# Twenty-five node tiles in the first gather stage, and the first sum of squares formed by TensorE

## The chip, the cores and the metric

The kernel runs on one core of a Trainium2 chip. The metric is the device time of the whole program in microseconds. Engines are named as in the profile: PE (TensorE, with PEld for its weight loads), DVE (VectorE), ACT (ScalarE), POOL (GpSimd, which issues the indirect gathers) and SP (SyncE, which issues the plain transfers).

## The reference

A chain of four graph layers over x (100000 nodes, 64 features) with 25000 edges; after each layer stands a layer norm of x plus the layer's output:

```python
x = _layernorm(x + _L0_gnn_ref(x, ..., src, dst))
x = _layernorm(x + _L1_gnn_ref(x, edge_attr_2, src, dst, ...))
x = _layernorm(x + _L2_gnn_ref(x, edge_index, ...))
x = _layernorm(x + _L3_gnn_ref(x, edge_index, ...))
```

Most nodes receive no edge. For those the layers' outputs are simple: layer 0 gives relu(b_ffn), layer 1 gives zero, layer 2 gives a linear map of the node's own state plus a bias, layer 3 gives zero. So their four norms shrink to a dense path with two sums of squares. The nodes that are some edge's dst need the real sums; they are few, and are written over the dense result at the end.

## The kernel before

**Edges** are sorted by dst and handled in 25 edge tiles of 1024 (NS = 25, SE = 1024; the last has 424 edges in its first half only, so its gather is 4 indirect transfers where the others have 8). A state tile is 128 x 512: two edges' 64 features on the partitions, or one edge row of 8 x 64 on each partition. **Nodes** are handled in 98 node tiles of 1024.

The program is a row of stages, each a block with a barrier at its end. Names as in the code:

- The stage S (setup) and the stage SA (up to about 600 us): gather x by src and dst, dense path for the src states, sums by dst, a lookup.
- S0 (c_, from 601 to 886 us): gather from table[0] (8 indirect transfers for each edge tile, line 461), gate with an exp, segment sum by two scans (lines 472 and 476), ffn matmul (line 1150), norm (lines 491 to 526), and back to features on partitions (line 533). No node tile here.
- S1 (d_, 886 to 1217 us): gather from table[1], moments and logits of layer 1, and beside them the first 50 node tiles, two for each edge tile (`paced`).
- S2, the softmax SF, and S3 (to 1438 us): no gather, no node tile.
- S4 (h_, 1438 to 1717 us): gather from table[2], logits of layer 2, and the other 48 node tiles.
- The softmax SI, S5, and S6 (gather and scatter, to the end).

**Orders.** Each engine's order within a stage is written out by `pipelined` (a slot for each edge tile) or `paced` (two slots for each edge tile, one for each node tile). In slot t, a step of depth d works on tile t - d. Every step is a generator; `yield v` gives it a place in the slot, and `merge` runs the pieces in order of v, older tiles first. So engines are strictly in order: a wait holds everything behind it. GA, GB, XN, W and the PSUM banks P have two halves (par 0 and 1), for even and odd tiles.

**A node tile before** (S1, S4): load from x (line 633), 4 transposes (467), vt = identity plus bias (653, ACT), `dense_pe`: 4 chunks against center and 4 against chain (610), both with nodes on the partitions of the output; Square (616), `dense_sum` (621, DVE: 128x512 to 128x8), sqrt (600), reciprocal (675), y0 (625), bias (627), Square (666), reduce (682), sqrt, reciprocal (685), product (688), store to out_x (638). An f32 matmul is two records in the profile, a transpose is one.

Lines the prediction follows in S0: 1108 product of states (DVE), 1118 V, 472/476 scans, 1150 ffn matmul, 1139 logit matmul, 1111 clip, 517 reduce of the norm, 526 its product, 1123 u, 1158/1166/1161 relu, relu and exp (ACT; exp and sqrt need different tables, so there are two ACT_TABLE_LOAD for each edge tile).

Of the kernel before, what the change touches and what calls it, by code (L numbers as in the profile page):

```python
# [143 lines left out]
def build(nc, a, out):  # L144
    ctx = ExitStack()
    with ctx:
# [354 lines left out]

        def keeping(dve, S):
            for par in range(2):
                dve.sem_inc(S(f"kept{par}"), 1)
# [23 lines left out]
        def back_dve(dve, T, s, par, k, step=1):  # L528
            yield step
            dve.wait_ge(T("x_fm"), k)  # L530


            dve.scalar_tensor_tensor(at(XD, s), at(MORE, s), 0.0, P[4 * par + 3][:, ::-1], A.is_equal, A.mult).then_inc(T("kept"), 1)
# [57 lines left out]

        def sm(par, k, n=1):
# [54 lines left out]
        def node_pe1(pe, T, n, par, k):  # L647
            yield from dense_pe(pe, T, par, k, 0)
# [22 lines left out]
        def node_dve2(dve, T, n, par, k):  # L671
            yield from dense_sum(dve, T, par, k, 0)
# [30 lines left out]
        def only(base, *stages):  # L703

            def of_node(stage):
                return lambda T, n, par, k: stage(T, n, par, k) if is_node(n, base) else None
            return [stage and of_node(stage) for stage in stages]

        def nodes_sync(sp, S, base, *owns):
# [12 lines left out]
            paced(sp, S, only(base, load, None, None, None, None, store), owns)  # L722
            count = min(NODES, NG + 1 - base)
            for par in range(2):
                sp.wait_ge(S(f"out_stored{par}"), 16 * ((count + 1 - par) // 2 + 1))

        def nodes_tensor(pe, S, base, *owns, unrolled=False):
            for par in range(2):
                pe.sem_inc(S(f"xn_free{par}"), 1)
            paced(pe, S, only(base, None, partial(node_pe0, pe), partial(node_pe1, pe)), owns, unrolled)  # L730

        def nodes_scalar(act, S, base, *owns):
            paced(act, S, only(base, None, partial(node_act0, act), partial(node_act1, act), partial(node_act2, act), partial(node_act3, act)), owns)

        def nodes_vector(dve, S, base, *owns):
            paced(dve, S, only(base, None, None, None, partial(node_dve2, dve), partial(node_dve3, dve)), owns)
# [361 lines left out]
        S0 = Sems("c_")  # L1098
        with nc.Block() as block:
# [5 lines left out]
            def _(dve):  # L1105
                def gate(T, s, par, k):
# [4 lines left out]
                    dve.tensor_scalar(W[par][2], P[4 * par + 1][:, :], -5.0, 5.0, A.max, A.min).then_inc(T("clipped"), 1)  # L1111

                def sums(T, s, par, k):
# [9 lines left out]
                    dve.tensor_tensor(W[par][4], at(XD, s), W[par][3], A.add).then_inc(T("u"), 1)  # L1123
                keeping(dve, S0)
                pipelined(dve, S0, gate, sums, partial(norm_dve, dve), partial(back_dve, dve))

# [655 lines left out]
```

## Time and profile before

| | before |
|---|---|
| median of 3 runs (range) | 2573.97 us (2572.82 to 2577.59) |
| profiled execution, whole / span | 2577.51 / 2575.7 us |
| mean granted TensorE clock | 0.748 |
| busy share PE, PEld, DVE | 54%, 32%, 73% |
| busy share ACT, POOL | 31%, 55% |

The span runs from the first to the last instruction. The granted clock is a share of 2.4 GHz: 1.0 is 2.4 GHz and 0.5 is 1.2 GHz. A busy share over the whole span mixes the stages, which have different limits, so the views below are cut by stage.

### The profile page before, as it was taken

The page shows a single profiled execution, that of the slowest core. Times are in us where ns is not written, and L with a number is a line of the kernel's source. Part 1 is how long each engine was busy: PE and PEld are TensorE (multiplying, and loading weights), DVE is VectorE, ACT ScalarE, POOL GpSimd, SP SyncE. Part 2 cuts the span into 40 slices and gives each one's busy share as a digit, 9 for nine tenths or more (in the row PEclk, how much of TensorE's full clock was granted, in tenths as well). Part 3 has the DMA queues.
Part 4 walks back from the last instruction along what each step waited for, and adds up shares of the span by engine and source line. Part 5 has one row for each costly group of instructions (what it writes and reads, how often), then busy time and mean ns, then how long its engine had stood idle before and what let it go on. Part 6 is the DMA issues. An engine that isn't in the chain of part 4 may idle for free. (4 is left out here: it accounts for less than half of the span.)

```text
span 2575.7 us, 25825 instructions
## 1 busy us (share of the span) xinstructions
PE 1392.9 (54%) x5738; PEld 832.2 (32%) x5738; DVE 1867.6 (73%) x3900; ACT 791.9 (31%) x1636; POOL 1423.4 (55%) x1382
## 2 busy tenths in 40 slices
PE   1433444444666588887466577634888543333231
PEld 1332333331333354443233455421333221212120
DVE  3877777875767589998688699977888675455542
ACT  1222222222545355554122355531222110101010
POOL 6777777735777576662000577730000277777776
PEclk9656555555877699999688899976888666566666
DMA  5433333431111233332011244420000011101010
GB/s 176 119 110 108 110 104 98 119 91 33 52 44 49 58 102 106 108 105 74 20 39 39 87 128 127 127 78 16 31 27 27 28 23 23 25 23 24 22 22 13
DMA packets 120400, 174.79 MB, mean 68 GB/s; under 512 B 36128, under 2 KB 42382, under 8 KB 120340
## 3 DMA queue, kind: packets, MB, share of 16 engines
q1 hardware_dynamic: 74836, 129.98, 15.0%
q0 software_dynamic: 43904, 43.81, 8.6%
q10 hardware_dynamic: 1600, 0.33, 0.1%
q8 instruction: 22, 0.36, 0.1%
q14 instruction: 38, 0.31, 0.0%
HBM read 88.48 MB, written 86.74 MB: 68 GB/s over the span
## 5 line engine op out<-in xcount | busy, mean ns | idle before, releaser
L461 POOL DMA_INDIRECT GA<-table,look_i x588 | 608.0, 1034 | 493.5 <-PEq L1473 213.0
L467 PE MATMUL P<-ident,GA 128*128 128x128 f32 x500 | 105.3, 348 | 411.6 <-DMA GB<-in_x,dst_i 198.9
L491 PE MATMUL P<-center,work 128*128 128x128 f32 x800 | 152.1, 352 | 210.9 <-DVE work L1697 174.2
L266 POOL DMA_INDIRECT GA<-in_x,src_i x196 | 210.6, 1074 | 83.5 <-issue 70.8
L1637 POOL DMA_INDIRECT out_x<-work,seg_i x196 | 205.0, 1046 | 59.8 <-issue 59.5
L1629 POOL DMA_INDIRECT GA<-table,look_i x196 | 200.2, 1022 | 59.8 <-issue 59.4
L266 POOL DMA_INDIRECT GB<-in_x,dst_i x196 | 196.9, 1004 | 59.7 <-issue 59.7
L509 ACT ACTIVATE work<-P 128x512 f32<-128x512 f32 x100 | 59.7, 597 | 518.6 <-PE P L491 518.1
L491 PEld LDWEIGHTS P<-center,work 128*128 128x128 f32 x800 | 135.9, 257 | 242.2 <-issue 113.1
L467 PEld LDWEIGHTS P<-ident,GA 128*128 128x128 f32 x500 | 71.1, 176 | 441.7 <-issue 222.3
L610 PE MATMUL P<-center,work 128*128 128x128 f32 x984 | 160.6, 313 | 91.1 <-ACT work L653 67.4
L610 PEld LDWEIGHTS P<-center,work 128*128 128x128 f32 x984 | 136.2, 215 | 169.7 <-ACT work L653 96.5
L1641 POOL MEMSET GA<- 128x512 f32 x1 | 0.5, 524 | 339.7 <-SPq L1622 339.7
L610 PE MATMUL P<-chain,work 128*128 128x128 f32 x984 | 146.4, 298 | 0.0
L1003 DVE SCALAR_TENSOR_TENSOR work<-P,src_f,unit_row 128x200 bf16<-128x200 f32 x400 | 142.5, 422 | 0.4
L610 PEld LDWEIGHTS P<-chain,work 128*128 128x128 f32 x984 | 136.4, 215 | 0.0
L566 DVE TENSOR_TENSOR_SCAN work<-MORE,car,XD 64x512 f32 (+1 forms) x100 | 127.9, 1279 | 8.2 <-DVEq L556 0.7
L908 PE MATMUL P<-step_up,work 128*128 128x201 bf16 x400 | 72.7, 358 | 102.6 <-DVE work L1003 98.2
L517 DVE TENSOR_REDUCE small<-work 128x8 f32<-128x512 f32 x100 | 68.4, 684 | 73.7 <-ACT work L509 72.9
L467 PE MATMUL P<-ident,work 128*128 128x128 f32 x400 | 81.9, 342 | 68.9 <-DVE work L526 67.0
L1599 PE MATMUL P<-work,wh 128*128 128x512 f32 x200 | 114.9, 713 | 1.5
L600 ACT ACTIVATE small<-small,vec 128x8 f32<-128x8 f32 x221 | 65.1, 295 | 141.8 <-DVE small L682 123.4
(332 smaller groups left out, 3448.9 us busy)
## 6 DMA issues: line engine op xcount, KB each, us to landing
table<-work SPq DMA_DIRECT2D x175, 256.0 KB, 2.4
XN<-in_x SPq DMA_DIRECT2D x98, 256.0 KB, 2.7
out_x<-work SPq DMA_DIRECT2D x98, 256.0 KB, 2.4
GA<-table,look_i POOLq DMA_INDIRECT x784, 2.4
XN<-in_src_pad SPq DMA_DIRECT2D x13, 512.0 KB
cols<-in_dst_pad SPq DMA_DIRECT2D x50, 128.5 KB, 4.7
table<-XN SPq DMA_DIRECT2D x1, 6400.0 KB
src_wide<-in_src_pad SPq DMA_DIRECT2D x12, 512.0 KB, 5.4
```

What stands on the lines that cost most here:

```text
L266: pool.indirect_dma_start(buf[:, s % 2, j * D:(j + 1) * D], None, a["x"], bass.IndirectOffsetOnAxis(ap=look[:, s * 8 + j:s * 8 + j + 1], a ...
L461: pool.indirect_dma_start(GA[:, par, j * D:(j + 1) * D], None, table_k, bass.IndirectOffsetOnAxis(ap=look[:, s * 8 + j:s * 8 + j + 1], axis=0)
L467: ins = pe.transpose(dst[:, q * 128:(q + 1) * 128], src[:, q * 128:(q + 1) * 128], ident[:, :])
L491: ins = pe.matmul(norm_bank(par, far)[:, q * 128:(q + 1) * 128], W[par][4][:, q * 128:(q + 1) * 128], center[:, :], start=True, stop=True)
L517: dve.tensor_reduce(small[:, par, 0:8], rows(W[par][5]), AX, A.add).then_inc(T("variance"), 1)
L566: dve.tensor_tensor_scan(B[lo:hi, ::-1], more, x, car[lo:hi, :], A.mult, A.add).then_inc(S(f"back{h}"), 1)
L610: ins = pe.matmul(p[:, q * 128:(q + 1) * 128], VT[:, q * 128:(q + 1) * 128], w[:, :], start=True, stop=True)
L908: ins = pe.matmul(block_of(par, q), steps(par)[:, h * HW + q * 128:h * HW + (q + 1) * 128], step_up[:, part, 0:RC + 1], start=(part == 0), ...
L1003: ins = dve.scalar_tensor_tensor(W[par][spare].bitcast(BF16)[:, q * RC:(q + 1) * RC], block_of(par, q)[:, 0:RC], src_f[:, col], unit_row[: ...
L1599: pe.matmul(P[4 * par][:, :], wh[g][:, :], W[par][g], start=(g == 0), stop=(g == HEADS - 1)).then_inc(T("head_sum"), 1)
L1629: pool.indirect_dma_start(GA[:, par, j * D:(j + 1) * D], None, table[3], bass.IndirectOffsetOnAxis(ap=look_i[:, r * 8 + j:r * 8 + j + 1], ...
L1637: pool.indirect_dma_start(out, bass.IndirectOffsetOnAxis(ap=seg_i[:, r * 8 + j:r * 8 + j + 1], axis=0), W[par][6][:, j * D:(j + 1) * D], N ...
```

## The change

1. **25 node tiles move to S0.** Node tiles 1, 3, ..., 49 are done in S0, one beside each edge tile. In S1 `even=True` keeps only the even ones of the first 50 (the odd steps aren't issued). S4 keeps its 48.
2. **Banks are shared in S0.** The gate has P[1] for both parities (its first matmul waits until the tile before has been clipped), the transposes back have P[3] for both; P[5] and P[7] are the node tiles' NA and NB. Node states are in XN (NX) and GB (NV).
3. **The first sum of squares, for all 98 node tiles.** The center matmul has center as its weights and the 512 columns of vt as the moving side: features on partitions. Square goes over that. `row_sums` then takes each chunk of 128 columns of the squares as weights and two columns of `total` as the moving side: 4 matmuls, 8 sums on each partition, in PSUM, where ACT's sqrt reads them. The DVE reduce of line 621 is gone for node tiles.
4. **In S0 new steps on each queue**: SP a load at the slot's start, which waits for `node_ss1` of two tiles before, and a store at place 4; ACT's `node_start` waits for `node_stored`.

```diff
+        def row_sums(pe, dst, squares):
+            for q in range(4):
+                ins = pe.matmul(dst[:, 2 * q:2 * q + 2], squares[:, q * 128:(q + 1) * 128], total[:, 0:128:64], start=True, stop=True)
+            return ins
         def node_pe1(pe, T, n, par, k):
-            yield from dense_pe(pe, T, par, k, 0)
+            VT = W[par][0]
+            yield 0
+            pe.wait_ge(T("vt"), k)
+            if not (isinstance(k, int) and k == 1):
+                pe.wait_ge(T("y0"), k - 1)
+            pe.matmul(BN[par][1], center[:, :], VT, start=True, stop=True).then_inc(T("dense_mm"), 1)
+            for q in range(4):
+                ins = pe.matmul(BN[par][2][:, q * 128:(q + 1) * 128], VT[:, q * 128:(q + 1) * 128], chain[:, :], start=True, stop=True)
+            ins.then_inc(T("dense_mm"), 1)
+        def node_pe2(pe, T, n, par, k):
+            yield 0
+            pe.wait_ge(T("sq1"), k)
+            row_sums(pe, BN[par][1], W[par][1]).then_inc(T("ss1"), 1)
         def node_act2(act, T, n, par, k):
             yield 1
             act.wait_ge(T("ss1"), k)
-            double_root(act, T, par, 2, 0, "sd1")
+            act.activation(sm(par, 2), BN[par][1][:, 0:8], ACT.Sqrt, scale=(1.0 + EPS) / D, bias=eps_2).then_inc(T("sd1"), 1)
         def node_dve2(dve, T, n, par, k):
-            yield from dense_sum(dve, T, par, k, 0)
             yield 2
...
+                def node_first(T, s, par, k):          # S0, DVE, with the norm of tile s
+                    yield 5
+                    dve.wait_ge(T("node_sd1"), k)
+                    dve.reciprocal(sm(par, 4), sm(par, 4)).then_inc(T("node_r1"), 1)
...
+                    dve.tensor_tensor(rows(NV[par]), rows(NB), per_row(sm(par, 4)), A.mult).then_inc(T("node_y0"), 1)
...
+                                      A.add).then_inc(T("node_y"), 1)
+                def node_second(T, s, par, k):         # S0, DVE, with the way back of tile s
+                    yield 1
+                    dve.wait_ge(T("node_sq2"), k)
+                    dve.tensor_reduce(sm(par, 5), rows(W[par][5]), AX, A.add).then_inc(T("node_ss2"), 1)
+                    yield 3
...
+                    dve.tensor_tensor(rows(NV[par]), rows(NV[par]), per_row(sm(par, 6)), A.mult).then_inc(T("node_out"), 1)
...
+                def node_turn(T, s, par, k):           # S0, PE
+                    yield 5
+                    pe.wait_ge(T("node_x"), 16 * k)
...
+                        pe.wait_ge(S0(f"node_sd1{older}"), turn)
+                    transpose4(pe, NA, NX[par]).then_inc(T("node_xt"), 1)
+                def node_dense(T, s, par, k):
+                    yield 1
...
+                    pe.wait_ge(T("node_vt"), k)
...
+                    pe.matmul(NA, center[:, :], NV[par], start=True, stop=True)
+                    for q in range(4):
+                        ins = pe.matmul(NB[:, q * 128:(q + 1) * 128], NV[par][:, q * 128:(q + 1) * 128], chain[:, :], start=True, stop=True)
+                    ins.then_inc(T("node_mm"), 1)
+                    yield 4
+                    pe.wait_ge(T("node_sq1"), k)
+                    row_sums(pe, NA, NX[par]).then_inc(T("node_ss1"), 1)
...
+                def node_start(T, s, par, k):          # S0, ACT, with the sums of tile s
+                    yield 6
+                    act.wait_ge(T("node_xt"), k)
+                    act.wait_ge(T("node_stored"), 16 * k)
+                    act.activation(NV[par], NA, ACT.Identity, bias=relub).then_inc(T("node_vt"), 1)
+                def node_first(T, s, par, k):          # ACT: Square at 2, sqrt of node_ss1 at 4
...
+                def node_second(T, s, par, k):         # ACT: Square of y at 0, sqrt of node_ss2 at 2
...
+                def node_load(T, s, par, k):           # S0, SP, depth 0
+                    yield 0
+                    if not (isinstance(k, int) and k == 1):
+                        sp.wait_ge(T("node_ss1"), k - 1)
+                    sp.dma_start(NX[par], rows_of(a["x"], (2 * s + 1) * SE)).then_inc(T("node_x"), 16)
+                def node_store(T, s, par, k):          # depth 3
+                    yield 4
+                    sp.wait_ge(T("node_out"), k)
+                    sp.dma_start(rows_of(out, (2 * s + 1) * SE), NV[par]).then_inc(T("node_stored"), 16)
```

(The words behind # in the diff are put in here to say where a step stands.)

## Rows read from the trace of the kernel before

**Rows 1.** Windows by stage (S0, S1, S4): length, busy PE, PEld, DVE, ACT, POOL, clock, DMA, GB/s.
```profile
610.00:875.00 265.00, 170.60 (x528) 88.15 (x528) 184.64 (x287) 129.34 (x166) 196.05 (x190) 0.77 0.18 46
890.00:1215.00 325.00, 268.63 (x1349) 154.76 (x1348) 282.18 (x549) 187.07 (x476) 201.88 (x194) 0.97 0.35 101
1438.00:1706.00 268.00, 185.04 (x1156) 130.65 (x1156) 238.91 (x429) 143.65 (x309) 200.92 (x196) 0.97 0.43 121
```

**Rows 2.** Groups by line, S0 from 620 to 860 us: busy, mean ns, idle before.
```profile
L461 POOL DMA_INDIRECT GA<-table,look_i x178 | 184.4, 1036 | 56.0 <-issue 56.0
...
L1118 DVE TENSOR_TENSOR work<-P,work 128x512 f32<-128x512 f32 x22 | 15.2, 692 | 38.9 <-PE P L467 38.9
```

**Rows 3.** Groups by line, S1 from 900 to 1200 us.
```profile
L461 POOL DMA_INDIRECT GA<-table,look_i x186 | 195.1, 1049 | 85.2 <-issue 51.6 <-PEq L1223 33.6
...
L610 PE MATMUL P<-center,work 128*128 128x128 f32 x384 | 56.6, 292 | 29.5 <-ACT work L653 22.5 <-PE P L1245 6.9
...
L621 DVE TENSOR_REDUCE small<-work 128x8 f32<-128x512 f32 x48 | 32.7, 681 | 0.0
...
L653 ACT ACTIVATE work<-P,vec 128x512 f32<-128x512 f32 x48 | 32.5, 677 | 0.0
...
L666 ACT ACTIVATE work<-work 128x512 f32<-128x512 f32 x47 | 29.4, 626 | 0.0
```

**Rows 4.** Groups by line, S4 from 1450 to 1690 us.
```profile
L461 POOL DMA_INDIRECT GA<-table,look_i x180 | 184.0, 1022 | 56.2 <-issue 56.2
...
L610 PE MATMUL P<-center,work 128*128 128x128 f32 x360 | 52.7, 291 | 43.5 <-ACT work L653 41.5 <-PE P L467 1.8
```

**Rows 5.** All of line 1118: min/median/max ns, first and last start.
```profile
L1118 DVE TENSOR_TENSOR work<-P,work x25: 690/692/693, 614.5 to 871.6; 128x512 f32<-128x512 f32 x25
```

**Rows 6.** Timeline, PE: first and last transposes of a gathered tile, S1, then S4.
```profile
898.60 1.12 PE L467 MATMUL P<-ident,GA 128*128 128x128 f32 x4 [3.02 <-DMA GA<-table,look_i]
...
1197.58 0.63 PE L467 MATMUL P<-ident,GA 128*128 128x128 f32 x4 [0.30 <-PE P L467]
...
1451.40 0.90 PE L467 MATMUL P<-ident,GA 128*128 128x128 f32 x3 [4.04 <-DMA GA<-table,look_i]
...
1702.62 0.66 PE L467 MATMUL P<-ident,GA 128*128 128x128 f32 x4 [0.84 <-DMA GA<-table,look_i]
```

**Rows 7.** Timeline, one slot of S0: start, length, engine.
```profile
740.58 0.68 DVE L1108 TENSOR_TENSOR work<-XS,XD 128x512 f32 x1
...
741.18 0.68 DVE L533 SCALAR_TENSOR_TENSOR XD<-MORE,P 128x512 f32 x1
...
742.76 0.69 DVE L1118 TENSOR_TENSOR work<-P,work 128x512 f32<-128x512 f32 x1 [0.90 <-PE P L467]
...
746.53 1.79 PE L1150 MATMUL P<-work,wffn 128*128 128x512 f32 x2 [2.63 <-DVE work L476]
...
746.69 0.69 DVE L517 TENSOR_REDUCE small<-work 128x8 f32<-128x512 f32 x1
...
750.06 0.69 DVE L1111 TENSOR_SCALAR work<-P 128x512 f32<-128x512 f32 x1 [0.30 <-PE P L1139]
```

**Rows 8.** Timeline of S1: a node tile on DVE, and a 512-column matmul at full clock.
```profile
1024.45 0.19 DVE L675 RECIPROCAL small<-small 128x8 f32<-128x8 f32 x1
...
1024.67 0.69 DVE L625 TENSOR_TENSOR work<-P,small 128x512 f32<-128x512 f32 x1
...
1025.40 0.69 DVE L627 TENSOR_TENSOR work<-work,bias_row 128x512 f32<-128x512 f32 x1
...
1029.39 1.10 PE L1231 MATMUL P<-XS,wfc 128*128 128x512 f32 x2
```

**Rows 9.** Line 1034, two stores of 256 KB one after the other: issue (ns), landing (us).
```profile
L1034 SPq DMA_DIRECT2D table<-work x50: 332/377/450, 77.1 to 580.2; - x50
...
DMA to landing us min/median/max: 2.1/2.8/3.4
```

**Rows 10.** Line 1380, the two records of one matmul with two moving columns: min/median/max ns.
```profile
L1380 PE MATMUL P<-red,fold x2: 355/365/375, 1219.5 to 1219.7; 128*128 128x2 f32 x2
```

More of the change, by code:

```diff
@@ L701, in first_of, with only, nodes_sync @@
             return N - SE if is_last(n, base) else (n + base) * SE
-        def only(base, *stages):
+        def only(base, *stages, even=False):
             def of_node(stage):
-                return lambda T, n, par, k: stage(T, n, par, k) if is_node(n, base) else None
+                return lambda T, n, par, k: stage(T, n, par, k) if is_node(n, base) and not (even and par) else None
             return [stage and of_node(stage) for stage in stages]
-        def nodes_sync(sp, S, base, *owns):
+        def nodes_sync(sp, S, base, *owns, even=False):
             def load(T, n, par, k):
@@ L1098, in build, with tile_before @@
         S0 = Sems("c_")
+        NX, NV = ([g[:, par, :] for par in range(2)] for g in (XN, GB))
+        NA, NB = P[5][:, :], P[7][:, :]
+        def tile_before(par, k):
+            return 1 - par, k - 1 + par
         with nc.Block() as block:
@@ L1132, in gate @@
                 def gate(T, s, par, k):
-                    bank = P[4 * par + 1][:, :]
+                    bank = P[1][:, :]
                     yield 1
                     pe.wait_ge(T("product"), k)
+                    if not (isinstance(s, int) and s == 0):
+                        older, turn = tile_before(par, k)
+                        pe.wait_ge(S0(f"clipped{older}"), turn)
                     pe.matmul(bank, proj[:, :], W[par][0], start=True, stop=True).then_inc(T("cos"), 1)
@@ L1157, in gate @@
                     act.wait_ge(T("cos"), k)
-                    act.activation(W[par][1], P[4 * par + 1][:, :], ACT.Relu, scale=inv_scale).then_inc(T("relu"), 1)
+                    act.activation(W[par][1], P[1][:, :], ACT.Relu, scale=inv_scale).then_inc(T("relu"), 1)
                     yield 5
@@ new lines, in node_second @@
+                def node_second(T, s, par, k):
+                    yield 0
+                    act.wait_ge(T("node_y"), k)
+                    act.wait_ge(T("variance"), k)
+                    act.activation(W[par][5], NV[par], ACT.Square).then_inc(T("node_sq2"), 1)
+                    yield 2
+                    act.wait_ge(T("node_ss2"), k)
+                    act.activation(sm(par, 6), sm(par, 5), ACT.Sqrt, scale=(1.0 + EPS) / D, bias=eps_2).then_inc(T("node_sd2"), 1)
+                pipelined(act, S0, gate, together(sums, node_start), together(partial(norm_act, act), node_first), node_second)
@@ L1171, in _ @@
                 storing(sp, S0)
-                pipelined(sp, S0, None, None, lambda T, s, par, k: store_table(sp, T, table[1], s, par, k, 6))
+                for par in range(2):
+                    sp.sem_inc(S0(f"node_stored{par}"), 16)
+                pipelined(sp, S0, node_load, None, lambda T, s, par, k: store_table(sp, T, table[1], s, par, k, 6), node_store)
                 all_stored(sp, S0)
+                sp.wait_ge(S0("node_stored0"), 16 * (NS // 2 + 2))
+                sp.wait_ge(S0("node_stored1"), 16 * (NS // 2 + 1))
```

58 lines of the change are left out of this document (40 added, 18 removed).

## The prediction

> **What bounds the kernel now.** A share over the whole span says little here, so I read the stages first [rows 1], then the groups by line within the three that change. In S0 the gathers set the pace: POOL's idle time in 240 us is all "issue", the short pause between two gathers, and there is no wait for a buffer; a gather and its pause take (184.4 + 56.0)/178 = 1.35 us [rows 2]. DVE waits there: 38.9 us for the transposes of the gathered tile [rows 2]. From the first V to the last, 24 edge tiles take 871.6 - 614.5 = 257.1 us, 10.71 each [rows 5]. S4 is the same, (184.0 + 56.2)/180 = 1.33 us a gather and nothing else in POOL's idle time [rows 4]; from the first to the last transposes (1702.6 - 1451.3)/24 = 10.47 us a tile (the last tile has half the gathers) [rows 6]. S1 is different: POOL waits 33.6 us until PE has freed a buffer [rows 3], and a tile takes (1197.58 - 898.60)/24 = 12.46 us [rows 6]; DVE is busy 282 of 325 us, head and tail included, and PE 269 [rows 1]. So S1 has two node tiles too much for the pace of its gathers, and S0 has room: 185 of 265 us on DVE, 171 on PE.
>
> **S1, what is taken away.** A node tile costs DVE two reduces, y0, bias and product, and two reciprocals: 5 x 0.69 + 2 x 0.2 = 3.85 us, by 0.68 us for a reduce [rows 3] and 0.69 and 0.19 us for the others [rows 8]. One of the two goes, and the other loses its reduce: 4.5 of 12.46 us, leaving about 8. PE loses a node tile: its center part is 56.6/48 = 1.18 us [rows 3], chain the same, transposes half, so 3 us. For the other, center becomes one matmul of 512 columns, 1.10 us [rows 8] for 1.18, and row_sums is added. Its price is not in the trace in this form. Bounds: the eight chunk records of center take 1.18 us with 128 moving columns each, and less can't be more, so 1.2 is the upper end at full clock; the two records with two moving columns took 0.36 us each, overlapping, at half clock [rows 10], so eight would be 1.6 us there and 0.8 at full clock. I take 0.8 to 0.9, by the row of the same shape; the lower end is nothing, if the loads hide under other matmuls. PE has then about 9.5 us of work for an edge tile, from 268.6/25 = 10.7 [rows 1]. Both are under the gathers' pace, so S1 falls to what S4 shows, 10.47 us: 24 x (12.46 - 10.47) = **-48 us**. If PE's waits add up to 11 us a tile it is -35.
>
> **S4.** Its gathers bound it and 48 reduces less on DVE (33 us of work) bring nothing. PE gets 1.7 us more for an edge tile, on 185/25 = 7.4 [rows 1]; but it waits 41.5 us, nearly 2 us a tile, for vt before the center matmul [rows 4], and row_sums stands right before that wait and needs only the Square that ACT does before vt. So it fills a wait: **+1 us**, between -2 and +12.
>
> **S0, what is added on DVE.** Per edge tile: reciprocal, y0, bias, reduce, reciprocal, product. Operations that don't hang on each other start 0.60 us apart (740.58 to 741.18 [rows 7]), dependent ones 0.73 (1024.67 to 1025.40), a reciprocal and its follower 0.22 [rows 8]. Slot by slot the new order is: product 0.60, way back 0.60, node reduce 0.65, V to the ffn matmul 3.77 (742.76 to 746.53 [rows 7]), copy 0.16, reduce 0.62, node reciprocal and product 0.84, norm's reciprocal and product 0.88, u 0.61, clip 0.61, then node reciprocal, y0 and bias 1.56: 10.9 us. That alone would be 0.2 over the gathers' 10.7, nearly free.
>
> **S0, the wait that is added.** SP is in order. Its load for tile t waits for row_sums of tile t - 2, which PE reaches late in slot t, behind ffn and logit. Behind that load stands the store of tile t - 3, whose data has been ready since the product. And ACT's node_start in the same slot waits for that store to have landed, since it writes the same buffer; behind it on ACT stands the Square of y, for which DVE waits (the node reduce) before it may go on to V and the scans; and PE's ffn matmul needs the scans. That is a ring once round per slot:
> - row_sums done to load issued 0.2, its issue 0.4, store's issue begins 0.1 later; landing 2.8 us from there (2.1 to 3.4 for a pair of such stores [rows 9]): 3.5 us.
> - Identity 0.68 and Square 0.63 [rows 3], overlapping by 0.1, and the hand-over to DVE: 1.2 us.
> - node reduce to V 0.65, V to ffn 3.77: 4.4 us.
> - ffn and logit: 2.0 us at full clock (1.10 for one [rows 8], and the next begins before its end), row_sums 0.85, end of the last 0.15: 3.0 us.
> The sum is 12.1 us. At half clock ffn to clip takes 750.06 - 746.53 = 3.53 us [rows 7] and the ring is some 1.5 longer. PE's clock in S0 is 0.77 now [rows 1], and it falls when PE has waited through the scans, for 2.63 us [rows 7]; after the change PE has the node matmuls in front of the scans and waits about 1.9 us, so I take one slot in ten slow: **12.2 us** a tile. It holds for 22 intervals (before slot 3 no store is waited for): 22 x (12.2 - 10.7) = +33 us. At the end the last node tile runs its own chain behind the norm's center matmul: center and chain 2, Square 0.6, row_sums 0.9, root 0.3, three DVE steps 1.6, Square, reduce, root and product 2.3, store and landing 3.2, 11 us; the norm's own Square, reduce, root, product and store need some 5 from the same point, and vt comes a microsecond or two late. So the 27.0 us from the last V to S1's first transposes (871.6 to 898.6 [rows 5, 6]) grow by **+8 us**, an estimate. S0 together **+41 us**, from +13 (at 11.0 us) to +75 (at 13.7).
>
> ACT gets about 2.5 us for each tile on 129/25 = 5.2 [rows 1], none of it a new table load, since the new roots stand beside the old one and ahead of the exp; it is covered but for the ring. The shared gate bank waits for a clip that is a slot old: nothing. Gathers would run ahead of DVE and wait for buffers: nothing.
>
> **A rule against it.** Gathers keep 1.35 us each with DVE 70% busy in S0 and 1.33 with DVE 89% busy in S4 [rows 1, 2, 4]; DVE's work doesn't slow them, so S4's rate is used for S1. The Trainium skill (SBUF — State Buffer, Who interferes with whom) says that GpSimd and VectorE share a port pair as an exclusive lock, so gathers' descriptors can be held up by VectorE; by that rule S0 would lose more and S1 and S4 gain; the trace doesn't bear it out.
>
> **Sum.** -48 + 1 + 41 = -6 us. Profiled execution 2577.5 -> 2571.5; it lay 3.5 above the median, so against the median 2573.97 the forecast is 2568 us.
>
> **Rivals.**
> A. *The ring is longer: the clock.* If PE waits a little more than 1.9 us before ffn, it drops to half clock in most slots, as it does now in S0: ring 13.4 us, S0 22 x 2.7 + 8 = +67, net +20: 2594 us. It decides from a ring of about 13 us on. For it: clock 0.77 now, and a late landing (3.4 us) adds to it. Against: PE gets 4 us more work a slot.
> B. *The ring is hidden.* If the store lands early or SP's load isn't late, DVE's order bounds S0 at 11.1 us: +9 + 6 = +15, net -32: 2542 us. Against it is the order of SP's queue; for it, that each term is at most a tenth of a microsecond off only if nothing overlaps, and some may.
> C. *PE bounds S1 and S4.* row_sums at 1.2 us or more, with waits: S1 11.0, S4 10.9 us a tile: 41 - 35 + 10 = +16: 2590 us. For it: PE was 83% busy in S1. Against: it fills waits.
> D. *Gathers get faster where DVE is relieved.* If a gather and its pause took 1.25 us, S1 and S4 would lose 16 us more each: -38: 2536 us. The three stages' rates speak against it. (The rule of the Trainium skill's page above would give this.)
>
> **Chances.** Forecast 0.42 (its own range 2559 to 2577), A 0.20, B 0.15, C 0.13, D 0.04, something else (0.06, spread evenly). Between 2545 and 2596 lie the forecast, most of A and C, and the upper edge of B; what is left out is most of B, D and the far end of A, 0.19. A difference of 0.2%, 5 us, is about what a measurement of this kernel can tell from none. Faster by more than that: 0.23 of the forecast's, B, D and 0.01 of the rest, 0.43; within it 0.15 of the forecast's and 0.08 of A, C and the rest, 0.23; slower 0.34.
>
> **What would show it.** V (line 1118's successor) in S0 12.2 us apart, ACT's Identity in S0 held by the landing of the store, DVE's node reduce held by ACT; POOL in S0 with waits for buffers and in S1 without; S1's gathered transposes 10.5 us apart and S4's unchanged; S0's clock above 0.85; row_sums 0.8 to 0.9 us. If S0's pace is 11 us, the ring was mis-seen; if S1's is over 11, PE was.

## The result, and where the time went

| | before | after |
|---|---|---|
| median of 4 runs (range) | 2575.43 us (2572.82 to 2577.59) | 2623.74 us (2618.76 to 2629.97) |
| ratio, 95% interval | | 1.0185 [1.0165, 1.0205] |
| profiled execution, whole / span | 2577.51 / 2575.7 us | 2618.76 / 2616.9 us |
| mean granted TensorE clock | 0.748 | 0.753 |

The changed kernel is 1.85% slower; 2568 us were forecast, with 2596 as the upper end. Between the two spans lie 41.2 us; the medians lie 48.3 apart, since the profiled execution of before was the slowest of its four and that of after the fastest. The marks that the prediction named cut up the 41.2: the product V of S0 (line 1118 before, 1149 after), and the transposes of the gathered tiles.

```profile
L1149 DVE TENSOR_TENSOR work<-P,work x25: 678/680/692, 615.9 to 921.2; 128x512 f32<-128x512 f32 x25
...
954.16 1.11 PE L467 MATMUL P<-ident,GA 128*128 128x128 f32 x4 [3.37 <-DMA GA<-table,look_i]
...
1217.62 0.60 PE L467 MATMUL P<-ident,GA 128*128 128x128 f32 x4
...
1471.84 1.11 PE L467 MATMUL P<-ident,GA 128*128 128x128 f32 x4 [3.53 <-DMA GA<-table,look_i]
...
1745.44 0.63 PE L467 MATMUL P<-ident,GA 128*128 128x128 f32 x4
```

(All of line 1149 with its first and last start; then, in time, the first and last transposes of a gathered tile in S1 and in S4, of after.) Against [rows 5, 6]:

| stretch | before | after | difference | forecast |
|---|---|---|---|---|
| start to the first V | 614.5 | 615.9 | +1.4 | 0 |
| S0, first V to last | 257.1 (10.71 a tile) | 305.3 (12.72) | +48.2 | +33 |
| last V to S1's first transposes | 27.0 | 33.0 | +6.0 | +8 |
| S1, first transposes to last | 299.0 (12.46) | 263.5 (10.98) | -35.5 | -48 |
| to S4's first transposes | 253.8 | 254.2 | +0.4 | 0 |
| S4, first to last | 251.2 (10.47) | 273.6 (11.40) | +22.4 | +1 |
| the rest | | | -1.7 | 0 |

Three terms missed, all to the same side: S0 by 15 us, S1 by 12, S4 by 21. The last lies outside the forecast's bounds for it (-2 to +12) and is twice the 10 us that rival C had.

**S0 in the profile of after.** The ring that the prediction walked through is there. (A ring: each wait in it is ended by the one before, so that a turn takes the sum of its members.) One turn at full clock, from one ffn matmul to the next (start, length, engine; in brackets the idle time before and what ended it):

```profile
759.47 1.13 PE L1205 MATMUL P<-work,wffn 128*128 128x512 f32 x2 [1.97 <-DVE work L476]
...
761.29 0.95 PE L601 MATMUL P<-total,XN 128*128 128x2 f32 x8
...
762.52 0.35 SPq L1275 DMA_DIRECT2D XN<-in_x  x1
...
763.17 0.33 SPq L1280 DMA_DIRECT2D out_x<-GB  x1
...
766.41 0.69 ACT L1249 ACTIVATE GB<-P,vec 128x512 f32<-128x512 f32 x1 [1.92 <-DMA out_x<-GB]
...
767.65 0.69 DVE L1169 TENSOR_REDUCE small<-work 128x8 f32<-128x512 f32 x1 [1.56 <-ACT work L1263]
768.25 0.68 DVE L1149 TENSOR_TENSOR work<-P,work 128x512 f32<-128x512 f32 x1
...
774.50 1.70 PE L601 MATMUL P<-total,XN 128*128 128x2 f32 x8
```

The row sums end at 762.24, SP issues the load and then the store, ACT's bias waits until the store has landed, DVE's reduce waits for ACT, V for the reduce, and the next ffn starts at 771.97: 12.5 us. The last line is the row sums of the next turn, at half clock: 1.70 us for 0.95, and that turn takes 13.6 us. Grouped by line over 280 us of S0:

```profile
L461 POOL DMA_INDIRECT GA<-table,look_i x184 | 192.7, 1047 | 88.7 <-issue 53.6 <-PEq L1202 35.1
...
L1249 ACT ACTIVATE GB<-P,vec 128x512 f32<-128x512 f32 x22 | 15.1, 686 | 32.6 <-DMA out_x<-GB 32.6
...
L1169 DVE TENSOR_REDUCE small<-work 128x8 f32<-128x512 f32 x21 | 14.4, 685 | 31.7 <-ACT work L1263 31.7
```

POOL now waits 35.1 us for buffers, where it waited for none [rows 2]: the gathers have lost the lead to the ring.

**S4 in the profile of after.** Here POOL waits for nothing, before and after. The gathers themselves have become longer, 1145 ns for 1022 [rows 4]:

```profile
L461 POOL DMA_INDIRECT GA<-table,look_i x179 | 205.0, 1145 | 56.2 <-issue 56.2
```

The shortest gathers take 0.94 us, with a pause of 0.30 to 0.31 us, 1.25 together. I call **lost** what the 196 gathers of a stage take above 0.94 us each (184.2 us together). These are the windows around the gathers of S0, S1 and S4 (stretch, its length, POOL busy in gathers (number), clock, share of the DMA engines, GB/s), first of before:

```profile
601.60:865.40 263.80, 202.48 (x196) 0.76 0.18 46
886.60:1179.20 292.60, 204.59 (x196) 0.96 0.37 105
1438.80:1700.60 261.80, 200.92 (x196) 0.97 0.43 122
```

and of after:

```profile
603.20:900.20 297.00, 204.74 (x196) 0.86 0.29 78
942.80:1208.70 265.90, 204.97 (x196) 0.92 0.28 73
1458.80:1742.90 284.10, 222.85 (x196) 0.92 0.40 113
```

S4 lost 16.7 us before and 38.6 after; the window grew by 22.3 us, busy time by 21.9. In both, length less busy time is 61 us, the pauses. What holds a gather is beside it in the timeline of S4. DVE and POOL, after:

```profile
1602.56 0.69 DVE L639 TENSOR_TENSOR work<-work,bias_row 128x512 f32<-128x512 f32 x1
...
1602.68 1.40 POOL L461 DMA_INDIRECT GA<-table,look_i  x1 [0.30 <-issue]
...
1604.12 1.28 DVE L572 TENSOR_TENSOR_SCAN work<-MORE,car,XD 64x512 f32 x1
...
1604.38 1.79 POOL L461 DMA_INDIRECT GA<-table,look_i  x1 [0.30 <-issue]
...
1605.73 1.27 DVE L572 TENSOR_TENSOR_SCAN work<-MORE,car,XD 64x512 f32 x1
...
1606.48 1.30 POOL L461 DMA_INDIRECT GA<-table,look_i  x1 [0.30 <-issue]
```

and before, where the kernel has a reduce ahead of the scans:

```profile
1520.78 0.68 DVE L621 TENSOR_REDUCE small<-work 128x8 f32<-128x512 f32 x1
1521.49 1.28 DVE L566 TENSOR_TENSOR_SCAN work<-MORE,car,XD 64x512 f32 x1
...
1523.11 1.28 DVE L566 TENSOR_TENSOR_SCAN work<-MORE,car,XD 64x512 f32 x1
```
```profile
1522.46 1.08 POOL L461 DMA_INDIRECT GA<-table,look_i  x1 [0.30 <-issue]
1523.85 1.31 POOL L461 DMA_INDIRECT GA<-table,look_i  x1 [0.30 <-issue]
```

A gather that begins while DVE is inside one of these instructions ends 0.8 us after it: 1602.56 + 0.69 = 1603.25, and the gather ends at 1604.08; the scan ends at 1605.40, the gather at 1606.17; the next at 1607.00 and 1607.78; before, the scan at 1522.77 and the gather at 1523.54. What is lost depends on how early in DVE's instruction the gather begins: 0.26 us behind the scan's start costs 0.85 us, 0.97 us behind it 0.14. After the change the bias addition pushes the train of gathers so that the next begins right behind the scan's start. Over the whole stage, counted by the DVE instruction under way when each gather of 1 us or more began, scans held 46 gathers for 12.2 us before and 46 for 25.7 after; the bias addition and the other product held 11 for 2.3 us before and 40 for 11.4 after.

The theory: S0 is the ring; S4 is gathers held back by DVE instructions with two inputs in SBUF, and the change moved only the moments at which they meet. Rivals: S0's added work, S4's PE (rival C of the prediction), or something that the first stages leave for S4.

### The profile page after: what moved, and what is told of

The parts are those of the page before. It is cut to its first block and busy times, and to the rows that moved or that the text cites. A ratio compares the mean times of both kernels' runs of the same rounds, so it can differ in the third digit from the quotient of the medians.

```text
span 2616.9 us, 26206 instructions
## 1 busy us (share of the span) xinstructions
PE 1477.6 (56%) x5934; PEld 886.9 (34%) x5934; DVE 1811.9 (69%) x3802; ACT 796.1 (30%) x1636; POOL 1450.0 (55%) x1382
## 5 line engine op out<-in xcount | busy, mean ns | idle before, releaser
L461 POOL DMA_INDIRECT GA<-table,look_i x588 | 632.6, 1076 | 521.4 <-PEq L1587 215.2
L491 PE MATMUL P<-center,work 128*128 128x128 f32 x800 | 153.0, 353 | 217.0 <-DVE work L1811 178.5
L1743 POOL DMA_INDIRECT GA<-table,look_i x196 | 200.0, 1021 | 59.8 <-issue 59.4
L491 PEld LDWEIGHTS P<-center,work 128*128 128x128 f32 x800 | 136.8, 258 | 244.1 <-issue 117.7
L472 DVE TENSOR_TENSOR_SCAN work<-SAME,car,work 64x512 f32<-64x512 f32 (+1 forms) x75 | 95.8, 1277 | 13.4 <-DVE work L1552 9.1
L476 DVE TENSOR_TENSOR_SCAN work<-SAME,car,work 64x512 f32<-64x512 f32 (+1 forms) x75 | 96.3, 1284 | 8.2
L667 PEld LDWEIGHTS P<-chain,work 128*128 128x128 f32 x584 | 85.5, 211 | 39.9 <-issue 39.9
L665 PE MATMUL P<-work,center 128*128 128x512 f32 x146 | 88.9, 693 | 16.4 <-ACT work L678 9.3
L526 DVE RECIPROCAL small<-small 128x8 f32<-128x8 f32 x100 | 19.7, 197 | 109.7 <-ACT small L518 108.9
```

The lines of the kernel that those rows point to most:

```text
L461: pool.indirect_dma_start(GA[:, par, j * D:(j + 1) * D], None, table_k, bass.IndirectOffsetOnAxis(ap=look[:, s * 8 + j:s * 8 + j + 1], axis=0)
L472: dve.tensor_tensor_scan(F[0:64, :], m[0:64, :], V[0:64, :], car[0:64, :], op0, op1).then_inc(T("scan0"), 1)
L476: dve.tensor_tensor_scan(F[64:128, :], m[64:128, :], V[64:128, :], car[64:128, :], op0, op1).then_inc(T("scan1"), 1)
L491: ins = pe.matmul(norm_bank(par, far)[:, q * 128:(q + 1) * 128], W[par][4][:, q * 128:(q + 1) * 128], center[:, :], start=True, stop=True)
L665: pe.matmul(BN[par][1], center[:, :], VT, start=True, stop=True).then_inc(T("dense_mm"), 1)
L1743: pool.indirect_dma_start(GA[:, par, j * D:(j + 1) * D], None, table[3], bass.IndirectOffsetOnAxis(ap=look_i[:, r * 8 + j:r * 8 + j + 1], ...
```

## The experiments

Ratios are against the kernel before on the same chip; its median was 2579 us beside e1 to e4 and e5 to e7, and 2580 beside e8 to e10. us a tile is over 24 intervals, from the marks above; lost is POOL's, as defined. Both come from one profiled execution of each kernel, which lay up to 7.4 us from its kernel's median (e3's was the fastest of eight, e8's the slowest of four).

| | median us | ratio, 95% interval | S0, S1, S4 us a tile | lost S0, S1, S4 |
|---|---|---|---|---|
| before | 2575.4 | | 10.71, 12.46, 10.47 | 18, 20, 17 |
| after | 2623.7 | 1.0185 [1.0165, 1.0205] | 12.72, 10.98, 11.40 | 20, 21, 39 |
| e1_s4_old | 2598.9 | 1.0089 [1.0065, 1.0112] | 12.56, 10.95, 10.47 | 21, 21, 17 |
| e2_load_late | 2576.5 | 0.9993 [0.9982, 1.0004] | 11.00, 10.81, 11.40 | 21, 20, 38 |
| e3_both | 2557.0 | 0.9923 [0.9903, 0.9943] | 10.98, 10.96, 10.57 | 21, 23, 19 |
| e4_moved_only | 2591.0 | 1.0055 [1.0036, 1.0074] | 12.54, 10.90, 10.47 | 27, 22, 17 |
| e5_sums_only | 2610.0 | 1.0120 [1.0097, 1.0143] | 10.63, 12.92, 11.52 | 16, 27, 40 |
| e6_idle_reduce | 2558.4 | 0.9919 [0.9890, 0.9948] | 10.99, 10.98, 10.58 | 21, 24, 17 |
| e7_moved_late | 2566.7 | 0.9952 [0.9933, 0.9971] | 11.45, 10.97, 10.54 | 31, 24, 18 |
| e8_sums_s0_only | 2552.8 | 0.9893 [0.9873, 0.9912] | 11.21, 10.89, 10.54 | 27, 22, 17 |
| e9_scan_psum | 2558.7 | 0.9920 [0.9902, 0.9938] | 11.23, 11.00, 10.46 | 14, 24, 17 |
| e10_bias_psum | 2545.3 | 0.9859 [0.9834, 0.9883] | 11.31, 10.47, 10.68 | 11, 11, 22 |

### e1_s4_old: S4's sums back on DVE

```diff
-nodes_tensor(pe, S4, NODES, (2, states), (3, logits))
+nodes_tensor(pe, S4, NODES, (2, states), (3, logits), old=True)
```

With old=True the stages on PE, ACT and DVE are dense_pe, double_root and dense_sum, as in the kernel before.

> The changed kernel with one part undone: in S4 alone the node tiles are as before (eight centring and chain matmuls with rows on partitions, the first sum of squares by a DVE reduce, none by PE). Theory (S4's +22.3 us comes from POOL's gathers being held longer once the sums have left DVE and its two-SBUF-input instructions stand at other moments): the interval between S4's gathered transposes returns from 11.40 us to 10.5, POOL's mean gather there from 1145 ns to 1020 to 1050, the time is 2600 us (2597 to 2606). Rival (S4 is slower because of something that the first stages left, or the clock in that stage): S4 stays at 11.3 to 11.4 us a tile and the time at 2618 to 2628.

```profile
1458.10:1719.70 261.60, 200.76 (x196) 0.97 0.43 122
```

S4's window is that of before to 0.2 us, though all that precedes it is as in the changed kernel; the median fell by 24.8 us. So S4's loss comes from how S4's own node tiles are summed, and not from what the first stages leave.

### e2_load_late: the ring opened

```diff
 def node_load(T, s, par, k):
-    yield 0
+    yield 5
```

> The changed kernel, but in S0 SP issues the load of a node tile's rows behind the store of the tile three older (place 5 in its slot, not 0), so the store no longer stands behind a load that waits for row sums. Theory (the ring row sums, load issue, store issue, landing, ACT bias, matmuls, squares, row sums sets S0's 12.7 us): S0's interval falls to 10.9 to 11.4 us, its 24 intervals by 32 to 44 us, ACT's wait for the output store (32.6 us in 280) goes nearly to nothing, the time is 2584 us (2578 to 2594). Rival 1 (the added work on PE and DVE makes S0 longer, the wait only shows it): 12.5 to 12.7 us a tile, 2618 to 2626. Rival 2 (the ring closes again through the late load and PE's transposes of it): 12.0 to 12.5 us a tile, 2605 to 2618.

The gathers' window in S0, and ACT's bias grouped over 620 to 870 us:

```profile
601.90:870.00 268.10, 205.66 (x196) 0.95 0.33 90
```
```profile
L1249 ACT ACTIVATE GB<-P,vec 128x512 f32<-128x512 f32 x23 | 15.4, 669 | 0.0
```

The wait for the store is gone, 32.6 us to nothing, and S0 is 41 us shorter for one changed place in SP's order; no work was taken away. Length less busy time is 62 us, so POOL waits for no buffer. DVE hardly waits either: 3.2 us in the 220 from 640 to 860 us, where it waited 54 in the kernel before. Most intervals between two V are 10.76 and 10.94 us, which is the gathers' pace (8 x 1.25 us and what they lose) and DVE's own order at once. The clock in this window is 0.95, 0.86 in after. The median fell by 47.3 us, to just under my range; the 41 us of the intervals lie in theirs.

### e3_both: the two together

(Both diffs.)

> The two edits together: S0's load behind the store, and S4's node tiles as before. S1 keeps sums by PE. Theory: the two gains add, S0 -36 and S4 -22 to -24 against the changed kernel, which gives 2564 us (2556 to 2574), faster than the kernel before by 0.4%. Rival (the stages are not independent, a gain in one is given back in the next): above 2580.

The gains add to within their scatter: 66.7 us against 47.3 + 24.8 = 72.1 (the intervals of these ratios are 0.1 to 0.2% wide to each side, 3 to 6 us). This kernel is faster than before by 0.8%.

### e4_moved_only: 25 tiles moved, no sums by PE

```diff
-    pe.matmul(NA, center[:, :], NV[par], start=True, stop=True)
+    for q in range(4):
+        pe.matmul(NA[:, q * 128:(q + 1) * 128], NV[par][:, q * 128:(q + 1) * 128], center[:, :], start=True, stop=True)
...
-    row_sums(pe, NA, NX[par]).then_inc(T("node_ss1"), 1)
+    dve.tensor_reduce(sm(par, 3), rows(NX[par]), AX, A.add).then_inc(T("node_ss1"), 1)
```

(In S0; S1 and S4 as S4 in e1.)

> 25 node tiles in S0 as in the changed kernel, but every first sum of squares by a DVE reduce from rows on partitions, in S0, S1 and S4 (one half of the change alone). The load stays ahead of the store in S0. Theory: S4 as in the kernel before, 10.5 us a tile (-22 us against the changed kernel); S0 keeps the ring, with a reduce of 0.6 to 0.7 us and its queueing on DVE in the place of row sums of 1.2 us: 12.2 to 13.0 us a tile; S1 10.3 to 10.6 us a tile if PE's row sums held it at 10.98, which gives 2588 us (2578 to 2605). Rival (S1's missing gain is due to POOL or to PE's other work, and not to the row sums): S1 stays at 10.9 to 11.0, the time is 2600 (2592 to 2612).

The total lies in the range, the theory's part on S1 fell: S1 stays at 10.90 us a tile without a single row sum on PE, so PE's row sums do not hold it there. POOL does: in this window too length less busy time is the pauses alone, and the rest is lost time.

```profile
937.00:1204.30 267.30, 206.39 (x196) 0.94 0.28 73
```

### e5_sums_only: the sums by PE in the kernel before

```diff
-paced(pe, S, only(base, None, partial(node_pe0, pe), partial(node_pe1, pe)), owns, unrolled)
+paced(pe, S, only(base, None, partial(node_pe0, pe), partial(node_pe1, pe), partial(node_pe2, pe)), owns, unrolled)
...
 def node_dve2(dve, T, n, par, k):
-    yield from dense_sum(dve, T, par, k, 0)
```

(With node_pe1, node_pe2 and node_act2 as in after, in S1 and S4.)

> The other half of the change alone: the kernel before with the first sum of squares of every node tile in S1 and S4 by PE, and no node tile in S0. Theory: S4 as in the changed kernel, 11.4 us a tile (+22 us); S1, with 49 node tiles, loses 0.69 us of DVE work for each of two node tiles a slot and gains 1.1 us of PE work for each, 12.46 us a tile becoming 12.2 to 12.7; the time 2595 us (2586 to 2606). Rival (the slow S4 comes from the node tiles moved ahead, that is from the state the first stages leave): S4 10.5 us a tile, 2568 to 2580.

Windows of S1 and S4:

```profile
887.00:1189.20 302.20, 211.35 (x196) 0.97 0.37 102
1450.30:1735.50 285.20, 223.88 (x196) 0.91 0.39 112
```

S4 has the changed kernel's loss (40 us lost) with nothing moved. S1 came out worse than I expected, by 11 us and not 0: 6.8 us of its window are longer gathers (211.35 for 204.59), the other 3 are about what POOL's waits for a buffer that PE frees have grown by (37.1 us for 33.6). The time, 2610, is above my range. By itself, the half of the change that moves work from DVE to PE costs 1.2%.

### e6_idle_reduce: more work on DVE

On e2, in S4 alone; the reduced column is read by nobody, the sums used are PE's.

```diff
 def node_dve2_idle(dve, T, n, par, k):
+    yield 0
+    dve.wait_ge(T("sq1"), k)
+    dve.tensor_reduce(sm(par, 7), rows(W[par][1]), AX, A.add).then_inc(T("idle"), 1)
     yield from node_dve2(dve, T, n, par, k)
```

> The kernel e2_load_late (2576.5 us) with one instruction more a node tile in S4: DVE waits for the squares and reduces them into a column that nobody reads, at the place where the kernel before formed its sum; PE's row sums stay and are what is used. It adds 0.69 us of DVE work to each of 50 tiles. Theory (S4's +22 us is where DVE's two-SBUF-input instructions fall against POOL's gathers, and DVE's schedule decides that): S4's interval goes from 11.41 us to 10.5 to 10.8, the time to 2558 us (2553 to 2565), faster by adding work. Rival 1 (PE's row sums and what waits for them hold S4): 11.4 us a tile, 2573 to 2582. Rival 2 (DVE is short of time there): 11.6 to 12.0 us, 2582 to 2592.

```profile
1415.20:1678.20 263.00, 201.00 (x196) 0.96 0.43 121
```

The trace has 48 of these reduces (not 50), of 0.68 us, and the kernel is 18 us faster than e2: S4's gathers lose 16.8 us, as before the change. PE's row sums are all still there, so they are not the cause (rival C for S4 falls), nor was DVE short of time. A reduce in that place keeps the instructions on both its sides where they do little harm: counted as above, scans hold gathers for 11.9 us where they held 25.6 in e2, and products for 2.3 where they held 10.8.

### m1_beside and m2_spread: the price by itself

Kernels of their own, which compute nothing of the reference: gathers by POOL, and DVE with one kind of instruction.

> A kernel of its own that computes nothing of the reference: nine phases of 32 gathers each by POOL (128 rows of 64 floats by an index column, as in the stages), with DVE idle, or running one kind of instruction throughout: a product of two SBUF tiles 128x512; the same with one input in PSUM; a reduce 128x512 to 128x8; a scan 64x512 with byte mask and values in SBUF; a scan with values in PSUM; a scaling of one SBUF tile; and last the product of two SBUF tiles and the SBUF scan, each followed by a pause as long as an ACT copy. Theory (a gather cannot be finished by POOL while DVE runs an instruction with two inputs in SBUF): alone 0.94 us, reduce and PSUM inputs below 1.05 us, two SBUF inputs without pause 1.3 us or more, the SBUF scan 1.5 us or more, the paused ones between. Rival (DVE's instructions have no part in it): all phases within 5% of the first.

Windows of two of its phases, the products of two SBUF tiles and the scans from SBUF, without pauses between them:

```profile
51.50:91.60 40.10, 30.19 (x32) 1.00 0.14 26
187.50:238.30 50.80, 40.90 (x32) 1.00 0.11 20
```

Both fell short of what was expected. The scans' phase has 40.90/32 = 1.28 us a gather, for 1.5 or more; the scans ended 13 us before the phase did, and the 22 gathers that began beside them took 1.43 us on average, half of them 0.94 and most of the others 1.93 to 1.98. The product cost nothing (30.19/32 = 0.943 us), for 1.3 or more. But two products took 1.25 us, and so did a gather with its pause: each gather began 0.60 us into a product, 0.08 us before its end. In the last two phases, with a pause behind each instruction, the products did hold gathers (20 of them took 1.02 to 1.06 us) and the scans held each that began beside them (1.40 to 1.64 us). Hence the second kernel, with pauses of changing length.

> Again 48 gathers a phase beside one kind of DVE instruction, now with a pause after each that ACT makes, of another length every time, so that gathers and instructions meet at every phase and not at one that repeats (in m1_beside both had a period of 1.25 us in some phases). Phases in order: POOL alone; product of two SBUF tiles; product with one input in PSUM; reduce; scan with byte mask and values in SBUF; scan with values in PSUM; scaling of one SBUF tile; ACT copies alone. Theory (a DVE instruction whose data inputs all come from SBUF holds back the gather that has just begun, until it ends, and 0.76 us more pass then; scans are the worst because they are the longest): mean gather 0.94 us alone and beside ACT, 0.94 to 0.96 beside the reduce and both PSUM forms, 1.03 to 1.15 beside the SBUF product, 1.15 to 1.35 beside the SBUF scan, 0.97 to 1.05 beside the scaling. Rival (only the scan with a byte mask does it, the product of two SBUF tiles does not, as its first phase in m1_beside seemed to say): product 0.94 to 0.96 us.

All eight phases, in the order given there (POOL busy, 48 gathers):

```profile
6.00:66.20 60.20, 45.42 (x48) 1.00 0.14 26
73.00:136.20 63.20, 48.15 (x48) 1.00 0.13 25
143.00:203.00 60.00, 45.29 (x48) 1.00 0.14 26
209.00:269.30 60.30, 45.27 (x48) 1.00 0.14 26
276.00:351.50 75.50, 60.88 (x48) 1.00 0.11 21
358.00:418.00 60.00, 45.28 (x48) 1.00 0.14 26
424.00:486.40 62.40, 47.08 (x48) 1.00 0.13 25
493.00:553.00 60.00, 45.28 (x48) 1.00 0.14 26
```

Divided by 48: alone 0.946 us, product of two SBUF tiles 1.003, product with PSUM 0.944, reduce 0.943, scan from SBUF 1.268, scan with values in PSUM 0.943, scaling of an SBUF tile 0.981, ACT alone 0.943. Two SBUF tiles or an SBUF scan hold gathers, and so does a scaling, 0.45 us long; with one of two inputs in PSUM, nothing does. The product's mean is below my range (1.03 to 1.15): only 7 of the 48 gathers were held, the longest for 1.44 us, and beside the products alone (54 of the phase's 63 us) the mean is 1.013. The scans held all 34 gathers that began while they ran, so their phase doesn't show every meeting either. One meeting in the phase of the scans:

```profile
280.46 1.28 DVE L60 TENSOR_TENSOR_SCAN O<-mask,zero,b_in 64x512 f32<-64x512 uint8 x1 [0.43 <-ACT Q L94]
281.09 1.40 POOL L71 DMA_INDIRECT G<-in_x,idx  x1 [0.30 <-issue]
```

The scan ends at 281.74, the gather at 282.49, 0.75 us later. The Trainium skill (SBUF — State Buffer, Who interferes with whom) has this as an exclusive lock on a port pair that GpSimd shares with VectorE, and says that a reduce never contends: the reduce's row agrees. It says as well that a VectorE instruction with two inputs in SBUF contends with a GpSimd instruction that reads SBUF, yet infers that such a product doesn't hold back the generation of descriptors; 48.15 for 45.3 us here says that it holds an indirect gather back.

### e7_moved_late and e8_sums_s0_only: where are sums by PE worth it?

e7 is e4 with S0's load late, e8 is e3 with S1's sums on DVE too. They differ in S0's sums alone.

> e4_moved_only (2591.0 us: 25 node tiles in S0, every first sum by a DVE reduce) with S0's load behind the store. Theory (the ring was the whole loss of S0, and the sums by PE bring nothing to either stage): S0 11.0 us a tile or less, S1 10.9, S4 10.5, the time 2550 us (2542 to 2558), as good as e3_both's 2557 or better. Rival (in S0 the sums by PE are worth their 0.69 us of DVE a tile): S0 11.5 to 11.7 us a tile, 2560 to 2570.

> e3_both (2557 us) with S1's node tiles as before too, so that PE forms the sums in S0 alone. Theory (S1 runs at the speed of POOL's gathers, 244 us and what they lose, whoever forms the sums): S1 10.9 to 11.0 us a tile and the whole within 5 us of e3_both, 2552 to 2562. Rival (the reduces give S1 more gathers held back, or DVE becomes late there): S1 11.3 us a tile or more, 2565 to 2575.

e8 came as expected, within 5 us of e3 by the medians. e7 did not: S0 takes 11.45 us a tile and the whole 2567 us, as its rival had it (11.5 to 11.7, 2560 to 2570). S0's windows, e7 and then e8:

```profile
598.20:874.60 276.40, 215.04 (x196) 0.90 0.32 87
```
```profile
599.30:872.40 273.10, 210.80 (x196) 0.93 0.32 88
```

Length less busy time is 61 and 62 us in both, so POOL waits for no buffer; e7's gathers lose 31 us and e8's 27, e3's 21 with the same S0 as e8. But gathers alone don't explain e7. This is the larger of the only two waits of DVE in e7 from 640 to 860 us (us in total, times, longest), the other is 0.3 us:

```profile
DVE work L1161 <- PE P L467: 1.6, 2, 1.1
```

DVE works through its order without a wait, and 18 of the 24 intervals are 11.35 to 11.49 us, 0.6 more than the 10.76 and 10.94 of e2 and e3: that is the reduce, which starts 0.6 us ahead of the next instruction. So in S0 DVE is short of time, and the sums by PE are worth their reduce there, as the rival said. In e8 14 of the 24 intervals are 11.4 to 11.9 us, and DVE waits 7.3 us in the same stretch, 5.8 of them for gathered tiles; there the meeting of gathers and DVE does decide, and it varies by some 6 us between the executions of e3 and e8, which are equal in S0. Of the 14 us between the medians of e7 and e8 these profiles show 6 in S0; the rest was not traced.

### e9_scan_psum and e10_bias_psum: operands moved to PSUM

```diff
-V, F = W[par][8], W[par][7]
+V, F = P[4 * par], W[par][7]
...
-dve.tensor_tensor(rows(Y), rows(BN[par][2]), per_row(sm(par, 2)), A.mult).then_inc(T("y0"), 1)
+dve.tensor_tensor(rows(BN[par][2]), rows(BN[par][2]), per_row(sm(par, 2)), A.mult).then_inc(T("y0"), 1)
...
-dve.tensor_tensor(rows(Y), rows(Y), bias_row...
+dve.tensor_tensor(rows(Y), rows(BN[par][2]), bias_row...
```

The first two lines are e9, in S0. The others are e10, which has e9's too; in S0 it does the same to NB, and PE waits for y where it waited for y0.

> e3_both (2557 us) with one operand of S0 moved: the product that feeds the segment scan is written over its own PSUM bank and the scan reads it there, not from SBUF. The same instructions in the same order, of the same sizes. Theory (in S0 too POOL's gathers set the pace: 245 us and the 21 us that they lose, 15 of them to scans from SBUF): the gathers lose 6 to 9 us, S0's interval goes from 10.98 us to 10.3 to 10.5, the time to 2544 us (2538 to 2550). Rival 1 (DVE's own chain is as long and takes over): 10.8 to 11.0 us, 2552 to 2562. Rival 2 (PSUM makes the product or the scan longer): above 2562.

> e9_scan_psum with one operand more moved in every stage that has node tiles: the first product of a node tile stays in its PSUM bank and the bias is added from there, so this addition has one SBUF input and not two; PE gets the bank back one instruction later. Theory: the gathers lose 2 to 3 us less in each of four stretches, 5 to 10 us in all: 2536 us (2530 to 2545). Rival (the bank that comes back later is what is then late, or the phase of the other instructions shifts to a worse place): 2545 to 2560.

S0 of e9: the group of the gathers, and all engines over 240 us (busy PE, PEld, DVE, ACT, POOL, then clock, DMA, GB/s):

```profile
L461 POOL DMA_INDIRECT GA<-table,look_i x177 | 179.7, 1015 | 61.1 <-issue 55.0 <-PEq L1214 6.1
```
```profile
620.00:860.00 240.00, 189.80 (x940) 129.23 (x938) 218.51 (x379) 161.59 (x256) 179.08 (x177) 0.92 0.34 92
```

Not one gather of S0 is held by a scan any more in e9 (in e3 scans held 14.8 us, counted by the DVE instruction under way when each long gather began), which is the mechanism shown in place. But products hold 13.1 us where they held 5.7, POOL has begun to wait for buffers, and DVE is busy 91% of the time. The median lies in the range of rival 1; S0's interval, 11.23 us, lies above all ranges. Fourteen of the 24 intervals are 10.72 to 10.91 us, DVE's own order, as rival 1 said. Six are 12.2 to 13.5 us, and in them the granted clock was down (0.66 over one of 13.4 us, 0.86 over one of 12.2, 1.00 in one of 10.9), so that S0's gathers stood at a clock of 0.89 on average where e3 had 0.95. Whether the lower clock made these intervals long or followed from their waits was not tried. e10's median, 2545.3 us, lies on the border between its range and its rival's. It pays off in S1, where it was not expected to be large:

```profile
900.60:1156.60 256.00, 195.05 (x196) 0.95 0.29 76
1403.60:1670.70 267.10, 205.81 (x196) 0.95 0.42 119
```

S1's gathers lose 11 us for 24 in e9, none of it to the bias addition any more, and its tile takes 10.47 us; S4 loses 4 us more than in e9. At 2545 us, 1.4% under the kernel before, it is the fastest of all; how much of that is luck in how the instructions meet in S1 was not tried.

## Why the prediction was wrong, step by step

**What bounds the stages**: right for S0, S1 and S4 of before. Wrong was what POOL's pace is. I read 1.35 and 1.33 us for a gather and its pause [rows 2, 4] as its speed; it is 1.25 us and 17 to 20 us a stage of meetings with DVE. The mean looked constant because the losses were alike, and not because they were none.

**S4 (+1 forecast, +22.4)**: "row_sums fills a wait" is right, e6 keeps it and has the old time. The step that failed is the one sentence that 48 reduces less on DVE "bring nothing". They were no neutral work: they are instructions that do not hold a gather (0.943 us beside them), and they stood next to scans that do; without them the gathers lost 38.6 us for 16.7. "DVE's work doesn't slow them, so S4's rate is used for S1" and "the trace doesn't bear it out" were drawn from two averages; the two gathers of 1.08 and 1.31 us in a tile of S4, shown above, spoke for the rule and were in the trace to be seen. Rival D had the mechanism, with the wrong sign: relieving DVE need not free the gathers, it moves them.

**S0 (+33 forecast, +48.2)**: the mechanism was right, the ring with all its members in their order, and e2 shows that it is all of the loss but 7 us. Two sizes were off. At full clock the ring took 12.38 us (mean of 11 intervals) and not 12.1: from the end of the row sums to ACT's bias 3.8 to 4.2 us (4.17 in the turn shown) for 3.5, with 3.0 us (median) as the store's landing; ffn to the end of the row sums 2.77 for 3.0; the rest to 0.1. That is some 6 us in 22 intervals. And in nine intervals of 24 PE ran all or part of these matmuls at half clock; they took 13.74 us on average, where I took one in ten: 9 x 1.36 = 12 us for 3. The share of slow turns was the weakest number of the sum, chosen and not read; rival A had the effect and took it for most turns.

**The tail of S0 (+8, +6.0)**: right.

**S1 (-48 forecast, -35.5)**: it went to the pace of its gathers, and POOL waits for no buffer, as forecast. Its gathers lose 20.7 us where S4's lost 16.7, 4 us. And the last tile, with 4 gathers for 8, is passed by PE 9.9 us after its last gather began, in S4 of before 3 us: the short tile saved nothing here; 7 us. (That the other engines still need a whole slot for it is the likely reason, not shown.) Rival C's guess, the row sums, is refuted by e4; they did take 24.0 us for 22 tiles, 1.09 each, and not 0.8 to 0.9. One sum slipped: PE's work for an edge tile is 10.7 - 3 - 0.1 + 0.85 = 8.5 us by its own terms and not 9.5 (measured after the change: 222.8/25 = 8.9), which changes nothing, since both are under the gathers' pace.

**DVE's own order in S0 at 10.9 us**: borne out. With the ring open (e2) most intervals are 10.76 and 10.94 us with next to no wait of DVE, and e9's stay at 10.72 to 10.91 though its gathers lose 7 us less. (Rival B then used 11.1 us for the same thing.) It is what S0 runs into once the ring is gone.

**"Gathers would run ahead and wait for buffers: nothing"**: right in effect; 35.1 us of waits in S0 are the ring's sign and not its cause.

## What to carry to other kernels

Where an in-order queue holds a load that waits for late work ahead of a store that is ready, follow what waits for the store: moving the load behind it was worth 47 us here, with no work saved. Read the pace of gathers by their shortest and not their mean, and look at what DVE has under way when a long one begins; where they bound a stage, a DVE instruction is priced by where its inputs lie, not by its length alone, and taking one away can cost time. See too how long DVE waits in the stage: where it doesn't, as in S0 of e7, its own order is a limit even though the gathers never wait for a buffer.

## What was unexpected of the hardware

- A useless reduce of 0.68 us beside each of 48 node tiles made the kernel 18 us faster (e6 against e2).
- An indirect gather on POOL takes 0.94 us, but where that is later it ends 0.75 to 0.84 us after a DVE instruction with two inputs in SBUF that was under way when it began (0.75 to 0.76 after most scans, 0.81 to 0.84 after products); a scan of 1.28 us thus stretches it to 1.79 us in S4 and to 1.98 us in m1. The same scan with its values in PSUM costs it nothing (0.943 us).
- Products of two SBUF tiles back to back cost gathers nothing (0.943 us) where both repeat every 1.25 us, and 6% where they do not: a probe whose two sides have one period measures one phase.
- Kernels with the same S0 differed there by 5.5 us over 24 intervals in the profiled executions (e3 10.98, e8 11.21 us a tile), with 21 and 27 us lost; one execution of each was profiled.
